# Combining six expert rows per token: one contiguous run per token, seven places to load into, half of the sum as matmuls

## The reference, cut to what matters

```python
_, selected_experts = jax.lax.top_k(masked_scores, K)          # K = 6
weights = jnp.take_along_axis(original_scores, selected_experts, axis=-1)
weights = weights / jnp.sum(weights, axis=-1, keepdims=True)
...
out = d[unsort_idx].reshape(T, K, H)                           # T = 1024, H = 256
expert_out = jnp.sum(out * weights[..., None], axis=1)
shared = jax.nn.silu(x @ sw_gate) * (x @ sw_up) @ sw_down
return (expert_out + shared).reshape(B, S, H)
```

## Time and profile before

| | us |
|---|---|
| three runs, median | 1879.2 (1877.37 to 1879.74) |
| the profiled execution, its own time | 1879.65 |
| its span, first to last instruction | 1877.9 |
| mean granted clock of PE, share of full | 0.951 |

### The profile page before, as it was taken

One profiled execution on the slowest core, in us unless ns is written; L12 is line 12 of the kernel. 1 busy time (PEld: TensorE's weight loads), 2 busy tenths in 40 slices (PEclk: granted clock), 3 DMA queues, 4 the chain that ended last, 5 costly groups with the idle time before them and its releaser, 6 DMA issues. The chain is left out here.

```text
span 1877.9 us, 41481 instructions
## 1 busy us (share of the span) xinstructions
PE 1699.2 (90%) x14533; PEld 1305.7 (70%) x14679; DVE 1413.8 (75%) x3752; ACT 1096.8 (58%) x2774; POOL 1099.4 (59%) x1718
## 2 busy tenths in 40 slices
PE   4799999999999999999999999978999997289988
PEld 3677777878787788777877887756555553139974
DVE  7898887888977878878778788757566664675646
ACT  6577777767777667767676676642133332173534
POOL 5678695686776957967768568300366663181210
PEclk8899999999999999999999999997999998596998
DMA  3210110011011000200010000445298994500100
GB/s 125 74 51 30 60 58 30 19 36 47 18 38 36 18 19 18 63 27 18 20 36 18 24 1 24 148 142 206 72 280 269 273 269 153 152 11 24 46 9 23
DMA packets 74649, 140.24 MB, mean 75 GB/s; under 512 B 10921, under 2 KB 44818, under 8 KB 74194
## 3 DMA queue, kind: packets, MB, share of 16 engines
q1 hardware_dynamic: 63634, 105.37, 18.4%
q0 software_dynamic: 9984, 30.42, 4.7%
q10 hardware_dynamic: 832, 1.84, 0.3%
HBM read 111.73 MB, written 25.86 MB: 73 GB/s over the span
## 5 line engine op out<-in xcount | busy, mean ns | idle before, releaser
L920 DVE TENSOR_TENSOR att_pT<-att_pT 128x512 bf16<-128x512 f32 (+1 forms) x512 | 321.0, 650 | 165.9 <-ACT att_pT L729 162.9
L565 PE MATMUL att_out<-att_V,att_pT 128*128 128x128 bf16 x5760 | 386.8, 219 | 13.9 <-DVE att_pT L920 12.1
L565 PEld LDWEIGHTS att_out<-att_V,att_pT 128*128 128x128 bf16 x5760 | 349.0, 98 | 40.7 <-DVE att_pT L920 24.3
L729 ACT ACTIVATE att_pT<-att_pT 128x512 bf16<-128x512 f32 (+1 forms) x512 | 278.0, 572 | 128.8 <-PE att_pT L551 128.8
L735 ACT ACTIVATE att_prob<-att_scores,att_negmax 128x512 f32<-128x512 f32 (+1 forms) x512 | 330.3, 655 | 17.3 <-DVE att_negmax L909 16.9
L542 PE MATMUL att_scores<-att_K,att_Q 128*128 128x512 bf16 (+1 forms) x1408 | 298.3, 359 | 7.1 <-DVE att_Q L881 0.4
L907 DVE TENSOR_REDUCE att_mx<-att_scores 128x1 f32<-128x512 f32 (+1 forms) x512 | 291.3, 630 | 0.7 <-PE att_scores L542 0.6
L551 PE MATMUL att_pT<-att_ident,att_prob 128*128 128x128 f32 x1920 | 274.2, 274 | 0.0
L542 PEld LDWEIGHTS att_scores<-att_K,att_Q 128*128 128x128 bf16 x1536 | 150.5, 98 | 143.9 <-issue 1.7
L551 PEld LDWEIGHTS att_pT<-att_ident,att_prob 128*128 128x128 f32 x1920 | 208.6, 141 | 0.8
L465 PE MATMUL att_aux<-att_wkv,att_kvT 128*128 128x256 bf16 x1350 | 167.2, 273 | 17.8 <-DVE att_aT L881 15.3
(11 more groups left out here) (342 smaller groups left out, 3230.2 us busy)
## 6 DMA issues: line engine op xcount, KB each, us to landing
moe_wa<-in_wa_l SPq DMA_DIRECT2D x80, 480.0 KB
att_wq<-wq_s SPq DMA_DIRECT2D x12, 512.0 KB, 3.7
att_wo<-wo_s SPq DMA_DIRECT2D x12, 512.0 KB, 3.8
moe_y<-y_s SPq DMA_DIRECT2D x8, 768.0 KB, 4.6
att_stage<-in_ctx_l SPq DMA_DIRECT2D x9, 512.0 KB, 4.3
near_s<-att_windows POOLq DMA_DIRECT2D x8, 576.0 KB, 5.6
win_near<-near_s SPq DMA_DIRECT2D x32, 144.0 KB
moe_wb<-in_wb_l SPq DMA_DIRECT2D x80, 48.0 KB
```

What stands on the lines that cost most here:

```text
L565: last = nc.tensor.matmul(out_ps[:, i % 2, :], pT[:, i % 2, a, k, :], V[:, par, k, w, :], start=(k, a, w) == (0, 0, 0), stop=(k, a) == (KT ...
L729: nc.scalar.activation(pT[:, i % 2, 0, 4 * j:4 * j + m, :], pT_ps[j % 2][:, 0:m, :], ACT.Copy).then_inc(s["pt_hi"], 1)
L920: nc.vector.tensor_tensor(pT[:, i % 2, 1, 4 * j:4 * j + m, :], pT_ps[j % 2][:, 0:m, :], pT[:, i % 2, 0, 4 * j:4 * j + m, :], ALU.subtract) ...
```

## The change

The row of a result is now `token * 6 + turn`, so a token's six rows are one run of 6 KB; a load reads it so. The loads have seven places: the two of `y6` and five in the weight ring `wa`, whose 8 by 960 numbers a lane hold five times 6 by 256. Only the eighth load waits, until the first tile is added up. ACT makes, in the job loop, 24 identity matrices scaled by a weight (8 tiles of tokens, 3 rows); PE multiplies them by rows 0 to 2 of a tile and adds in PSUM; DVE adds rows 3 to 5 as before and then PE's sum. Each load has a semaphore of its own. `token_table` takes four instructions instead of six.

```diff
+ON_PE = 3
+        IN_WA = WRING * WA // (TOPK * D)
+        HOMES, SUMS_OF = 2 + IN_WA, TOPK - ON_PE + 1
+        in_wa = wa[:, :, :].rearrange("p w n -> p (w n)")
+        def home(n):
+            n = n % HOMES
+            if n < 2:
+                return y6[:, n, :, :]
+            return in_wa[:, (n - 2) * TOPK * D:(n - 1) * TOPK * D].rearrange("p (k d) -> p k d", k=TOPK)
...
                 for n in range(TT):
-                    wait(sp, s["added"], SHARED + TOPK * (n - 1) if n > 1 else 0)
-                    rows = t["y_s"][0:UNUSED, :].rearrange("(k t) d -> t k d", k=TOPK)
-                    sp.dma_start(y6[:, n % 2, :, :], rows[n * P:(n + 1) * P]).then_inc(back[n % 2], 16)
+                    if n >= HOMES:
+                        sp.wait_ge(s["added"], SHARED + SUMS_OF * (n - HOMES + 1))
+                    rows = t["y_s"][0:UNUSED, :].rearrange("(t k) d -> t k d", k=TOPK)
+                    sp.dma_start(home(n), rows[n * P:(n + 1) * P]).then_inc(back[n], 16)
...
+                pe.wait_ge(s["share_scaled"], TT * ON_PE)
+                for n in range(TT):
+                    pe.wait_ge(back[n], 16)
+                    wait(pe, s["added"], SHARED + SUMS_OF * (n - 1) if n > 1 else 0)
+                    for k in range(ON_PE):
+                        last = nc.tensor.matmul(y_ps[n % 2][:, 0:D], scaled[:, n, k, :], home(n)[:, k, :], start=k == 0, stop=k == ON_PE - 1)
+                    last.then_inc(s["share_sum"], 1)
...
+                    if 0 <= j - SHARED - 16 < TT * ON_PE:
+                        n, k = divmod(j - SHARED - 16, ON_PE)
+                        if (n, k) == (0, 0):
+                            act.wait_ge(s["share_step"], 3 * TOPK)
+                        nc.scalar.activation(scaled[:, n, k, :], ident[:, :], ACT.Copy, scale=share[:, n, k:k + 1]).then_inc(s["share_scaled"], 1)
...
-                def add_row(q):
...
+                def add_rows(n):
+                    dve.wait_ge(back[n], 16)
+                    for m, k in enumerate(range(ON_PE, TOPK)):
+                        dve.wait_ge(s["added"], SHARED + SUMS_OF * n + m)
+                        V.scalar_tensor_tensor(x[:, n, :], home(n)[:, k, :], share[:, n, k:k + 1], x[:, n, :], ALU.mult, ALU.add).then_inc(s["added"], 1)
+                    dve.wait_ge(s["added"], SHARED + SUMS_OF * (n + 1) - 1)
+                    dve.wait_ge(s["share_sum"], n + 1)
+                    V.tensor_tensor(x[:, n, :], x[:, n, :], y_ps[n % 2][:, 0:D], ALU.add).then_inc(s["added"], 1)
...
-    scratch("y_s", [UNUSED + NSLOT * P, D], F32)
+    scratch("y_s", [UNUSED + TOPK + NSLOT * P, D], F32)
```

More of the change, by code:

```diff
@@ L1382, in experts @@
         share = sc.sb("share", [P, TT, TOPK])
+        scaled = sc.sb("scaled", [P, TT, ON_PE, P])
         hit = sc.sb("hit", [P, TT, E_ALL])
@@ L1388, in experts @@
                  "hot", "table_part", "table_ready", "rows_ready",
-                 "xt_done", "xt_sb", "up_done", "silu_done", "h_done", "ht_done", "ht_sb", "y_done", "y_sb", "added", "quant", "share_step"]
+                 "xt_done", "xt_sb", "up_done", "silu_done", "h_done", "ht_done", "ht_sb", "y_done", "y_sb", "added", "quant", "share_step", "share_scaled", "share_sum"]
         s = {n: sc.sem(n) for n in names}
-        load, stored, gathered, back = ([sc.sem(f"{n}{i}") for i in range(r)] for n, r in (("load", WRING), ("stored", YRING), ("gathered", XRING), ("back", 2)))
+        load, stored, gathered, back = ([sc.sem(f"{n}{i}") for i in range(r)] for n, r in (("load", WRING), ("stored", YRING), ("gathered", XRING), ("back", TT)))
         route(nc, t, x, h32, sel, selb, gates, wabs, wvo, [
@@ L1617, in token_table @@
                     V.tensor_scalar(token_row[:, :], token_ps[:, 0:NSLOT], float(EMPTY), None, ALU.add).then_inc(s["table_ready"], 1)
[L1618 to L1623, removed]
+                    V.scalar_tensor_tensor(spare[:, :], token_ps[:, 0:NSLOT], 0.0, const[:, CONST["spare"]], ALU.is_ge, ALU.mult)
+                    link(V.tensor_scalar(turn_no[:, :], token_ps[:, NSLOT:2 * NSLOT], float(TOPK * (EMPTY + 1)), None, ALU.add))
+                    link(V.scalar_tensor_tensor(turn_no[:, :], token_ps[:, 0:NSLOT], float(TOPK), turn_no[:, :], ALU.mult, ALU.add))
+                    V.tensor_tensor(result_row[:, :], turn_no[:, :], spare[:, :], ALU.add).then_inc(s["rows_ready"], 1)
                 def hidden(j):
@@ L1704, in _ @@
                 dve.wait_ge(s["share_step"], 3 * TOPK)
-                for q in range(TT * TOPK):
-                    add_row(q)
+                for n in range(TT):
+                    add_rows(n)
 def window_attention(nc, t, x, hhl, wabs, wvo):
```

## The result

The changed kernel takes 1865.8 us, median of four runs (1864.89 to 1866.96); the kernel before, on the same chip, 1878.35 (1877.37 to 1879.74). The ratio is 0.9933, 95% interval 0.9916 to 0.9950: 12.5 us less. 1868.6 was forecast, 1865.3 to 1873.3 as the range. The profiled execution took 1864.89, its span is 1862.8, and the mean granted clock of PE is 0.961 instead of 0.951.

What follows compares the result with a forecast made beforehand. The combine was taken as bound by DVE and the loads waiting for each other, with neither full. Loads at 2.23 us would end it at 1610.2, saving 11.0: 1879.65 less 11.0 is 1868.6, range 1865.3 to 1873.3.

Steps and rivals of the forecast that it cites:

- DVE, 2.1 us a tile: In the combine: three additions, hand-overs and one PSUM addition take DVE 2.1 us a tile instead of 3.09.
- Loads, 2.23 us each, the pace of the combine: In the combine: loads land 2.23 us apart at the earlier 354 GB/s, the eighth at 1607.4.
- the bound below: Earliest end of the combine, if only DVE limits: 1591.75 + 8 x 2.1 = 1608.6, saving 12.6 us.
- The end: End of the combine's last addition: 1607.4 + 2.3 + 0.1 + 0.42 = 1610.2 against 1621.23, saving 11.0 us.
- PE: Combine matmuls: 2.7 to 3.0 us a tile at half clock, 1.34 to 1.5 at full; rise near 1596 to 1598.
- Rival 1: In the combine, PE stays at half the clock and sets the pace: 7.2 us saved, 1872.4; chance 0.22.
- No limit on loads in flight: In the combine, seven loads are issued in a row unhindered, as SP issued 16 transfers in a row in 12.6 us.
- ACT: In the job loop, 24 scaled copies at about 0.29 us, 7 us in all, hidden in ACT's wait for PE.
- Rival 4: Job-loop scatters at wider addresses cost DMA more: gain gone at 2.2 times, 1899 at three times; chance 0.03.
- Rivals 2 and 3: Rival 2: the combine's loads do not overlap as thought, 3 us saved as a low case, 1876.6; chance 0.03.
- rival 3: Second attention: PE's clock returns one projection later, costing 13.1 us, 1881.7; steps 5.14 apart at half, 2.76 at full; chance 0.04.
- What follows: After the combine, all work moves 11 us forward; shifted clock changes add 1.5 us to both sides.

Runs made afterwards that it cites:

- the run that kept the clock up: Changed kernel plus unused bf16 matmuls of 512 columns on PE, 10 ahead of the second attention's first step, 5 in each of its first six: 1853.3 us, ratio 0.9869.

## Why the prediction was right, point by point

*What bounds it.* Load latency and additions in turn, with two places. Shown, with one part of it open: the layout alone gives 1.6 us and the places alone 2.8. Two parts together give 3.7 (layout and places), 1.6 (layout and PE's half) and 10.5 (places and PE's half), all three 12.5. PE's half alone was not run.

*DVE, 2.1 us a tile*: 2.09. *First landing 4.7 after the issue*: 4.2, and 4.3 in the run with the layout alone.

*Loads, 2.23 us each, the pace of the combine.* This step was wrong in size, and with it the last tile's path: 1.89. I had named 6 KB pieces as what could be faster and still took the rate of the 1 KB pieces, "the nearest row"; in the two runs with the old layout and seven places 345 and 351 GB/s came back. So DVE's 2.1 a tile set the end, as in the bound below. For the last tile the sum has 2.3 us from landing to PE's sum; PE took 1.56 (1605.45 to 1607.01), and DVE, which began that tile's additions at 1607.45, did not wait for it.

*The end*, 1610.2 forecast, was 1609.43, 11.8 us earlier than before instead of 11.0. It lies so near by luck, as other terms make it up. The bound below, 1608.6, had left out PE's slow start, for which DVE waits 2.03 us (1.52 and 0.51), and the first landing came 0.8 sooner than assumed. That its 12.6 is nearly the medians' 12.5 is chance too. Of the 2.8 us by which the forecast total is high, 1.3 is its starting point, 1879.65 where the median measured with the changed kernel is 1878.35.

*PE.* 2.7 to 3.0 us at half the clock: the first two tiles, 5.46 in all; 1.5 at the full: 1.56. A rise near 1596 to 1598: within 1596 to 1597. That it would fall again by the end was wrong for the changed kernel, where the waits are 0.3, and seen with the old layout. Rival 1, half the clock throughout, did not happen; with two places six tiles of eight ran so.

*No limit on loads in flight.* True for the changed kernel, whose seven issues take 3.5 us. The reason given, 16 unhindered issues, does not carry over to 1 KB pieces: see below.

*ACT.* 0.29 us a copy, 7 us in all: ACT's busy time rose by 7.2 and its idle ahead of the silu fell by 7.0. A copy's own record is 0.39 long, but it begins before the one ahead has ended. Hidden, so it changed nothing.

*Scatters, table, waits, semaphores at nothing*: the job loop did not change in DMA share (0.91 before and after, 0.92 in the changed kernel with the old layout) or in PE's records. Rival 4 is out. Rivals 2 and 3 did not happen; the price of rival 3, steps at 5.14 and 2.76, was seen from the other side in the run that kept the clock up, with steps 2.75 apart from 1691.63 to 1694.38.

*What follows, 1.5 us either way*: the spans of the profiled pair differ by 3.4 more than the start of the next stage explains, more than the 1.5 allowed; the medians by 0.8.

## What to carry to other kernels

Where a load, a wait and a vector chain take turns, price the parts together: here the layout alone gave an eighth and the places alone a fifth of what the three gave. Moving half of the sum to TensorE was worth 7 us of combine with loads running ahead and nothing without (34.0 against 33.3, both with two places and the new layout). Read the granted clock beside the busy share: PE was busy 37 of 37 us at 0.51, and keeping the clock up there saved 12.5 us in spite of the filling. The 37 to 41 us at half the clock followed idling of 2 to 3.5 us ahead of the first step; filling that gap alone moved the fall to the next wait. Before taking a rate from a row, ask whether the pieces in it have the size of those to come.

## What the runs showed of the hardware that I had not expected

How long SP's queue took to issue a load depended on the pieces. Five loads of 768 pieces of 1 KB kept it 9.00 us, five of 6 KB runs, of the same bytes, 2.65. With the places alone the first three issues took 0.39 to 0.55 us, the fourth some 1.5, and the last four 2.12 to 2.52, about the 2.24 in which a load was moved at 351 GB/s. So SP itself was held up from the fourth load on. It cost nothing that DVE saw in that run, where its additions had no gap.

Large runs moved 417 GB/s from HBM on this one core for 12 us at a DMA share of 1.01, the 1 KB pieces 351 at 1.09 (1589 to 1606 in the run with seven places alone).

A few microseconds of filling matmuls, ahead of the first step and in the first six, went with a granted clock of 1.00 where the changed kernel has 37 us at 0.50; with less filling the clock fell later, and 27 to 31 us ran at 0.50. And a PE that works without a gap can stay at 0.50: in the kernel before, 34 us of f32 matmuls of 72 and 128 columns, busy all the time, went by at that clock, and it rose only inside the projection of 256 columns behind them. In the combine of the changed kernel it rose after some 6 us of gapless work. What makes the difference is not shown.

```profile
1688.00:1722.00 34.00, 34.00 (x168) 31.75 (x167) 20.80 (x85) 12.74 (x32) 6.97 (x10) 0.50 0.07 19
```
